# Adding the weighted scan states to y: one unit per GpSimd instruction, or two

## The chip, the cores and the metric

The kernel runs on one core of one Trainium2 chip. The metric is the time of one execution on the device, in microseconds (us). The kernel before took 3660.17 us (median of 3 runs, 3656.47 to 3664.53).

## The reference

One layer on x of shape [8, 512, 512] (batch, sequence L, features D): a feed-forward block, a state-space block (Mamba), and the same feed-forward block again, each added to x, the feed-forward ones by half.

```python
x = x + 0.5 * ffn(layernorm(x))
x = x + mamba(layernorm(x))
x = x + 0.5 * ffn(layernorm(x))
# ffn: h = silu(x @ w_gate) * (x @ w_up); of each 4 neighbours of h the 2 largest by magnitude stay; h @ w_down
# mamba, per batch element, E = 1024 channels, N = 16 states:
h = exp(d_l[..., None] * A) * h + (d_l * u_l)[..., None] * b_l[:, None, :]   # over l = 0..511
y_l = einsum('ben,bn->be', h, c_l)
y = (y + u * W_D) * silu(skip);  out = y @ W_out.T
```

The change touches the two lines of the recurrence: h is scanned over l for each channel and state, and y is the sum over the 16 states of h times C.

## The kernel before

**Tiling.** Features stand on the 128 partitions and the 512 positions along the free axis, so a tile is 128x512 float32. The 1024 channels are 8 tiles e = 0..7, worked in two halves of 4 (HE = 4). A *unit* is one tile e and one state n: one scan over 512 positions. There are 64 units in a half, 128 in a batch element, 1024 in all, numbered u = 0..1023; within a half u runs over e fastest, so 4 units in a row belong to the four tiles of one state.

**A unit passes through four engines.** ScalarE writes exp(delta*A) to a PSUM bank `decay[u % 2]` (L838). GpSimd multiplies du by the row B into `scan_in` (L1322, `scan_input`). VectorE scans (L1201, `scan`), in place in the `decay` bank, and multiplies the states by the row C into `scan_out` (L1211, `times_c`). GpSimd adds that to the tile `y[:, e, :]` (L1333, `sum_states`). `scan_in` and `scan_out` are rings of RING = 4 tiles.

**What orders them.** Semaphores count finished units: `decay_ready`, `input_ready`, `state_ready` (scan done), `weighted_ready` (times C done), `sum_ready` (added to y). `scan_input(u)` waits for the scan of u-4 (its ring tile is free), `times_c(u)` waits for the sum of u-4, ScalarE's exponential of u waits for `times_c(u-2)`. On GpSimd the queue is `scan_input(u)`, `sum_states(u-4)`, `scan_input(u+1)`, `sum_states(u-3)`, and so on; GpSimd does little else between the first unit and the last.

**Beside it** TensorE runs the 512 products of the feed-forward blocks (L621 to L623: three matmuls for high and low parts) with "side jobs" between them: down-projections (L713, L697 to L702), the counting of the 2-of-4 choice (L684), projections of the Mamba block (L728 to L730, L741), means and variances. A plan in Python fixes all orders beforehand in *ticks*; `place_units` spreads the units over the ticks by the other work that VectorE has there. VectorE's own queue in a tick is: up to a quarter of the tick's units, then residual and selection work (L1158, L1168, L1176, L1186), and so on; within a quarter it is scan(u), times_c(u), scan(u+1), with other work between the last scan and its times_c.

**VectorE lines with both inputs in SBUF** also matter: `zlo` (L1134) and `xlo` (L1140), four in a row; the scaling of the normalised input (L1120, L1128); `y` times the gate (L1241, function `gate`, four in a row), which waits until all sums of its half are in; and delta times u (L1248, 2048 columns). The last gate (batch element 7, second half) stands before the last output projection (L741), the last normalisation and the last feed-forward block.

Of the kernel before, what the change touches and what calls it, by code (L numbers as in the profile page):

```python
# [19 lines left out]
B, L, D = 8, 512, 512  # L20
E, N, DT, DC = 1024, 16, 128, 4
I = 2048
P = 128
KD = D // P
KE = E // P
HE = KE // 2
# [4 lines left out]
GROUPS = 2 * N  # L31
HALF = N * HE
UNITS = 2 * HALF
RING = 4
BANKS = 2
EXP_LEAD = 1
MAINS = 2
# [4 lines left out]
ROWS = 3  # L42
# [216 lines left out]
def build(nc, x_in, ffn_w, down_w, mam_w, out_w, wdt_in, wbc_in, wd2_in, small_in, out):  # L259
    f32, r32, bf16 = mybir.dt.float32, mybir.dt.float32r, mybir.dt.bfloat16  # L260
    ALU, ACT = mybir.AluOpType, mybir.ActivationFunctionType
# [4 lines left out]
    with ctx:  # L266
        base_of = {}

        def sb(name, shape, dt=f32):
            base_of[name] = nc.sbuf_base  # L270
            return ctx.enter_context(nc.sbuf_tensor(name, shape, dt))

        def pb(name):
            return ctx.enter_context(nc.psum_tensor(name, [P, L], f32))
# [35 lines left out]
        y = sb("y", [P, KE, L])  # L310
        delta = sb("delta", [P, KE, L])
        du = sb("du", [P, KE, L])
        scan_rows = sb("scan_rows", [P, 2 * ROWS, L])
        rows = [scan_rows[:, 2 * k:2 * k + 2, :] for k in range(ROWS)]
        scan_in = sb("scan_in", [P, RING, L])
        scan_out = sb("scan_out", [P, RING, L])
        db = [scan_in[:, k, :] for k in range(RING)]
        pr = [scan_out[:, k, :] for k in range(RING)]
        cv = [sb(f"cv{k}", [P, L]) for k in range(2)]
        skb = sb("skb", [P, L])  # L320
# [15 lines left out]
        decay = [pb(f"decay{k}") for k in range(BANKS)]  # L336
# [24 lines left out]
        def wait_job(eng, key):  # L361

            eng.wait_ge(sem["side_ready"], index[key] + 1)

        def wait_selected(eng, s, j):

            wait_read(eng, ("win", s, j))
# [10 lines left out]
        def last_down(i):  # L378

            return ("down", EDGE[i], KD - 1)  # L380
# [445 lines left out]
        def _(act):  # L826
# [87 lines left out]
            def member_high(i, j):  # L914

                s = EDGE[i]
                if i:
                    wait_job(act, last_down(i - 1))
                if i == AHEAD_OF_SCANS:
                    act.wait_ge(sem["state_ready"], B * UNITS)  # L920
                    act.wait_ge(sem["sum_ready"], B * UNITS)
                wait_selected(act, s, j)
                nc.scalar.activation(hhi[:, j, :], h[s % 2][:, j, :], ACT.Copy).then_inc(sem["member_high_ready"], 1)  # L923

            def down_high(i, t):

                q = KD * i + t
                act.wait_ge(sem[f"down_loaded_{t}"], 16 * (EDGE[i] + 1))
                if q >= ROWS:
                    wait_job(act, ("down", EDGE[(q - ROWS) // KD], (q - ROWS) % KD))  # L930
                if i == AHEAD_OF_SCANS:
                    act.wait_ge(sem["sum_ready"], B * UNITS)
                nc.scalar.activation(wparts[q % ROWS][:, 0], wdown[t][:], ACT.Copy).then_inc(sem["down_high_ready"], 1)

            def copy_quarters(key):
# [165 lines left out]
        def _(dve):  # L1101
# [96 lines left out]
            def scan(u):  # L1198
                dve.wait_ge(sem["decay_ready"], u + 1)
                dve.wait_ge(sem["input_ready"], u + 1)  # L1200
                nc.vector.tensor_tensor_scan(decay[u % BANKS][:], decay[u % BANKS][:], db[u % RING][:], 0.0, ALU.mult,  # L1201
                                             ALU.add).then_inc(sem["state_ready"], 1)

            def times_c(u):
                m = u // HE
                if u % HE == 0:
                    dve.wait_ge(sem[f"rows_loaded_{m % ROWS}"], 16 * (m // ROWS + 1))
                dve.wait_ge(sem["state_ready"], u + 1)
                if u >= RING:
                    dve.wait_ge(sem["sum_ready"], u - RING + 1)  # L1210
                nc.vector.tensor_tensor(pr[u % RING][:], decay[u % BANKS][:], rows[m % ROWS][:, 1, :], ALU.mult).then_inc(sem["weighted_ready"], 1)  # L1211

            def begin(units):
# [20 lines left out]
                ins.then_inc(read_of(key) if k == DC - 2 else sem["conv_step"], 1)  # L1234

            def gate(b, half):
                dve.wait_ge(sem["sum_ready"], UNITS * b + HALF * (half + 1))
                dve.wait_ge(sem[f"skip_loaded_{half}"], 16 * (b + 1))
                for k in range(HE):
                    e = HE * half + k  # L1240
                    nc.vector.tensor_tensor(y[:, e, :], y[:, e, :], delta[:, gates_in(b, half).start + k, :],  # L1241
                                            ALU.mult).then_inc(sem["gated_ready"], 1)
# [67 lines left out]
        @block.gpsimd  # L1310
        def _(pool):
            def scan_input(u):
                b, v = divmod(u, UNITS)
                half, v = divmod(v, HALF)
                e, m = HE * half + v % HE, u // HE
                if v == 0:
                    pool.wait_ge(sem["du_ready"], 2 * b + half + 1)
                if u % HE == 0:
                    pool.wait_ge(sem[f"rows_loaded_{m % ROWS}"], 16 * (m // ROWS + 1))
                if u >= RING:  # L1320
                    pool.wait_ge(sem["state_ready"], u - RING + 1)
                nc.gpsimd.tensor_tensor(db[u % RING][:], du[:, e, :], rows[m % ROWS][:, 0, :], ALU.mult).then_inc(sem["input_ready"], 1)  # L1322

            def sum_states(u):
                b, v = divmod(u, UNITS)
                half, v = divmod(v, HALF)
                e = HE * half + v % HE
                if v == 0:
                    pool.wait_ge(sem["first_term_ready"], HE * (2 * b + half + 1))
                pool.wait_ge(sem["weighted_ready"], u + 1)  # L1330
                if v >= HE:
                    pool.wait_ge(sem["sum_ready"], u - HE + 1)
                nc.gpsimd.tensor_tensor(y[:, e, :], y[:, e, :], pr[u % RING][:], ALU.add).then_inc(sem["sum_ready"], 1)  # L1333

            def member_low(i, j):

                pool.wait_ge(sem["member_high_ready"], 4 * i + j + 1)
                nc.gpsimd.tensor_tensor(hlo[:, j, :], h[EDGE[i] % 2][:, j, :], hhi[:, j, :], ALU.subtract).then_inc(sem["member_split_ready"], 1)  # L1338

            def down_low(i, t):  # L1340

                w = wparts[(KD * i + t) % ROWS]
                pool.wait_ge(sem["down_high_ready"], KD * i + t + 1)
                nc.gpsimd.tensor_tensor(w[:, 1], wdown[t][:], w[:, 0], ALU.subtract).then_inc(sem["down_split_ready"], 1)

            nc.gpsimd.memset(ones[:], 1.0 / D).then_inc(sem["const_ready"], 1)
            nc.gpsimd.memset(pick[:], 0.0).then_inc(sem["const_ready"], 1)
            pool.wait_ge(sem["const_ready"], 2)
            for k in range(4):
                nc.gpsimd.memset(pick[2 * N * k:2 * N * k + 1, :], 1.0).then_inc(sem["const_ready"], 1)  # L1350
            pool.wait_ge(sem["const_ready"], 6)
            nc.gpsimd.memset(eps[:, 0:1], EPS).then_inc(sem["const_ready"], 1)
            nc.gpsimd.memset(eps[:, 1:2], EPS * EPS).then_inc(sem["const_ready"], 1)
            for k, sign in enumerate((1.0, -1.0)):
                nc.gpsimd.memset(signs[:, k, :], sign).then_inc(sem["const_ready"], 1)
                pool.wait_ge(sem["const_ready"], 2 * k + 9)
                nc.gpsimd.affine_select(signs[:, k, :], signs[:, k, :], pattern=[[-1, P]], compare_op=ALU.is_equal, fill=0.0, base=0,
                                        channel_multiplier=1).then_inc(sem["const_ready"], 1)
            nc.gpsimd.memset(fold[:], 0.0).then_inc(sem["const_ready"], 1)
            for k in range(4):  # L1360
                pool.wait_ge(sem["const_ready"], 13 + k)
                nc.gpsimd.affine_select(fold[:], fold[:], pattern=[[-1, 2 * N]], compare_op=ALU.not_equal, fill=1.0, base=-2 * N * k,
                                        channel_multiplier=1).then_inc(sem["const_ready"], 1)
            for tick in range(plan.ticks):
                if tick == STARTS[0]:
                    wait_job(pool, last_down(AHEAD_OF_SCANS - 1))
                for i, j in edge_members(tick):
                    member_low(i, j)
                for i, t in edge_weights(tick):
                    down_low(i, t)  # L1370
                for u in plan.units_at[tick]:
                    scan_input(u)
                    if u >= RING:
                        sum_states(u - RING)
                if tick == STARTS[B] - 1:
                    for u in range(B * UNITS - RING, B * UNITS):
                        sum_states(u)


def _tiles(v):  # L1380
# [36 lines left out]
```

## Time and profile before

| | before |
|---|---|
| median of 3 runs | 3660.17 us (3656.47 to 3664.53) |
| the profiled execution's own time | 3661.65 us |
| its span, first to last instruction | 3659.9 us |
| mean granted TensorE clock | 0.976 of full |
| TensorE matmul busy | 92% |
| VectorE busy | 83% |
| GpSimd busy | 74% |
| ScalarE busy | 56% |

The profile is one execution; its time is 1.5 us above the median. Scans run from about 300 to 3467 us; outside that GpSimd is nearly idle, so that within it its share is higher than the 74% of the whole. A matmul's recorded end is modelled, so that the share of TensorE is not a share of its peak. An instruction of an engine may be recorded as beginning before the one ahead of it has ended, by some hundredths of a microsecond.

### The profile page before, as it was taken

How to read it: one execution, taken by the hardware profiler on the slowest of the kernel's cores; microseconds unless marked ns; L12 is line 12 of the kernel's file. 1: busy time of each engine (PE TensorE's matmuls, PEld its weight loads, DVE VectorE, ACT ScalarE, POOL GpSimd, SP SyncE). 2: the span in 40 equal slices, each digit the busy share in tenths (PEclk: the TensorE clock that was granted, in tenths of full speed). 3: DMA queues.
4: the chain of work that ended last, by engine and by line, in shares of the span. 5: the costliest groups of instructions: out<-in, count | busy, mean ns of one | idle time of the engine just before them, and what ended most of it. 6: DMA issues, size and time to landing. Idle time of an engine off the chain costs nothing. (4 is left out here: it accounts for less than half of the span.)

```text
span 3659.9 us, 40068 instructions
## 1 busy us (share of the span) xinstructions
PE 3383.1 (92%) x11967; PEld 2131.8 (58%) x12032; DVE 3041.4 (83%) x3572; ACT 2060.4 (56%) x2803; POOL 2694.2 (74%) x2141
## 2 busy tenths in 40 slices
PE   8999999999999999899999999888988999898889
PEld 5775556556655665556555565556545565455466
DVE  5546888788889889898988899998989998989823
ACT  4546556557565664556555675656565665454332
POOL 1316776777888778787787788878988978989813
PEclk9999999999999999999999999999999999999999
DMA  9656556656656666466665575556645566546433
GB/s 350 212 187 191 159 203 210 217 164 216 206 170 216 187 219 216 150 205 206 190 201 178 188 232 185 180 163 214 222 125 207 167 219 202 175 150 187 129 109 104
DMA packets 243477, 696.51 MB, mean 190 GB/s; under 512 B 23536, under 2 KB 23792, under 8 KB 233584
## 3 DMA queue, kind: packets, MB, share of 16 engines
q1 hardware_dynamic: 173632, 559.72, 44.3%
q10 hardware_dynamic: 69632, 134.23, 14.2%
q8 instruction: 99, 1.62, 0.2%
q14 instruction: 114, 0.93, 0.1%
HBM read 619.94 MB, written 76.55 MB: 190 GB/s over the span
## 5 line engine op out<-in xcount | busy, mean ns | idle before, releaser
L1322 POOL TENSOR_TENSOR scan_in<-du,scan_rows 128x512 f32<-128x512 f32 x1024 | 1323.2, 1292 | 544.6 <-DVE decay L1201 456.1
L1333 POOL TENSOR_TENSOR y<-y,scan_out 128x512 f32<-128x512 f32 x1024 | 1351.4, 1320 | 104.7 <-DVE scan_out L1211 103.8
L1201 DVE TENSOR_TENSOR_SCAN decay<-decay,scan_in 128x512 f32<-128x512 f32 x1024 | 1252.2, 1223 | 147.9 <-ACT decay L838 137.0
L838 ACT ACTIVATE decay<-delta,aneg 128x512 f32<-128x512 f32 x1024 | 698.5, 689 | 1016.2 <-DVE scan_out L1211 1012.9
L621 PE MATMUL main<-zhi,wunit 128*128 128x512 f32 x2048 | 913.7, 446 | 129.8 <-ACT h L862 92.5
L623 PE MATMUL main<-zhi,wunit 128*128 128x512 f32 x2048 | 825.4, 403 | 0.0
L622 PE MATMUL main<-zlo,wunit 128*128 128x512 f32 x2048 | 824.5, 403 | 0.0
L713 PE MATMUL side<-h,wdown 128*128 128x512 f32 x1760 | 798.8, 598 | 8.4 <-DVE res_r L1186 3.3
L1211 DVE TENSOR_TENSOR scan_out<-decay,scan_rows 128x512 f32<-128x512 f32 x1024 | 702.7, 686 | 27.9
L621 PEld LDWEIGHTS main<-zhi,wunit 128*128 128x128 f32 x2048 | 394.6, 193 | 325.0 <-ACT h L862 131.0
L713 PEld LDWEIGHTS side<-h,wdown 128*128 128x128 f32 x1760 | 335.1, 192 | 374.6 <-issue 346.9
L622 PEld LDWEIGHTS main<-zlo,wunit 128*128 128x128 f32 x2048 | 396.1, 193 | 121.4 <-issue 37.3
L623 PEld LDWEIGHTS main<-zhi,wunit 128*128 128x128 f32 x2048 | 394.9, 193 | 97.0
L728 PE MATMUL side<-xhi,wmam 128*128 128x512 f32 x512 | 238.7, 466 | 43.7 <-DVE cv L1232 18.5
L1338 POOL TENSOR_TENSOR hlo<-h,hhi 128x512 fp32r<-128x512 f32 x36 | 48.4, 1367 | 282.4 <-ACT hhi L923 282.4
L838 ACT ACT_TABLE_LOAD x193 | 247.6, 1283 | 4.0 <-ACT skb L987 0.5
L741 PE MATMUL side<-y,wmam 128*128 128x512 f32 x512 | 232.2, 597 | 9.8 <-DVE y L1241 4.3
L1168 DVE TENSOR_TENSOR cmp<-ab,mag 128x512 bf16<-128x512 f32 (+2 forms) x192 | 232.5, 1211 | 10.2 <-ACT mag L871 8.9
L1158 DVE TENSOR_TENSOR h<-main,h 128x512 f32<-128x512 f32 x256 | 173.9, 679 | 53.6 <-PE main L623 53.6
L1176 DVE SCALAR_TENSOR_TENSOR h<-side,h 128x512 f32<-128x512 f32 x256 | 165.1, 681 | 60.7 <-PE side L684 60.5
L871 ACT ACTIVATE mag<-h 128x512 f32<-128x512 f32 x192 | 113.2, 589 | 179.7 <-DVE cmp L1168 118.0
L684 PE MATMUL side<-cmp,signs 128*128 128x512 bf16 x703 | 180.4, 391 | 33.0 <-DVE cmp L1168 14.5
(105 smaller groups left out, 3261.9 us busy)
## 6 DMA issues: line engine op xcount, KB each, us to landing
wunit<-hl_dram SPq DMA_DIRECT2D x480, 512.0 KB, 4.1
scan_rows<-bc_dram ACTq DMA_DIRECT2D x256, 512.0 KB, 5.5
wdown<-down_w_dram SPq DMA_DIRECT2D x256, 256.0 KB, 3.0
wmam<-mam_dram SPq DMA_DIRECT2D x128, 512.0 KB, 4.2
hl_dram<-wunit SPq DMA_DIRECT2D x32, 512.0 KB, 3.7
skip_dram<-skb SPq DMA_DIRECT2D x64, 256.0 KB, 4.2
delta<-skip_dram SPq DMA_DIRECT2D x16, 1024.0 KB, 8.1
wmam<-wout_dram SPq DMA_DIRECT2D x32, 512.0 KB, 4.4
```

The costliest lines, as they stand in the source:

```text
L621: nc.tensor.matmul(main[n % MAINS][:], hi[:, k, :], zhi[:, k, :], start=(k == 0), stop=False)
L622: nc.tensor.matmul(main[n % MAINS][:], hi[:, k, :], zlo[:, k, :], start=False, stop=False)
L623: mm = nc.tensor.matmul(main[n % MAINS][:], lo[:, k, :], zhi[:, k, :], start=False, stop=(k == KD - 1))
L713: mm = nc.tensor.matmul(bank[:], wdown[t][:, j, :], h[s % 2][:, j, :], start=(j == 0), stop=(j == 3))
L728: nc.tensor.matmul(bank[:], w[:, k, :], xhi[:, k, :], start=(k == 0), stop=False)
L741: mm = nc.tensor.matmul(bank[:], w[:, odd * KD + t, :].bitcast(f32), y[:, e, :], start=(c + odd == 0), stop=(c + odd == 2))
L838: nc.scalar.activation(decay[u % BANKS][:], delta[:, e, :], ACT.Exp, scale=aneg[:, e, n:n + 1]).then_inc(sem["decay_ready"], 1)
L1168: nc.vector.tensor_tensor(cmp[:, first:first + j, :], ab[:, 0:j, :], mag[:].unsqueeze(1).broadcast_to([P, j, L]), ALU.is_ge).then_inc(sem[ ...
L1201: nc.vector.tensor_tensor_scan(decay[u % BANKS][:], decay[u % BANKS][:], db[u % RING][:], 0.0, ALU.mult, ALU.add).then_inc(sem["state_read ...
L1211: nc.vector.tensor_tensor(pr[u % RING][:], decay[u % BANKS][:], rows[m % ROWS][:, 1, :], ALU.mult).then_inc(sem["weighted_ready"], 1)
L1322: nc.gpsimd.tensor_tensor(db[u % RING][:], du[:, e, :], rows[m % ROWS][:, 0, :], ALU.mult).then_inc(sem["input_ready"], 1)
L1333: nc.gpsimd.tensor_tensor(y[:, e, :], y[:, e, :], pr[u % RING][:], ALU.add).then_inc(sem["sum_ready"], 1)
```

## The change

GpSimd adds the weighted states of two units, which lie in neighbouring tiles of `scan_out`, to two neighbouring tiles of `y` in one instruction of 1024 columns. `sum_ready` now counts pairs, so each wait on it is halved. `scan_input` stays one instruction per unit. The GpSimd queue is now: `scan_input(u)` and `scan_input(u+1)` for an even u, then the sum of units u-4 and u-3.

```diff
-RING = 4
+INPUTS, RING = 4, 4
+
+LAG = 2
...
-        scan_in = sb("scan_in", [P, RING, L])
+        scan_in = sb("scan_in", [P, INPUTS, L])
...
             def times_c(u):
...
                 if u >= RING:
-                    dve.wait_ge(sem["sum_ready"], u - RING + 1)
+                    dve.wait_ge(sem["sum_ready"], (u - RING) // 2 + 1)
...
             def gate(b, half):
-                dve.wait_ge(sem["sum_ready"], UNITS * b + HALF * (half + 1))
+                dve.wait_ge(sem["sum_ready"], (UNITS * b + HALF * (half + 1)) // 2)
...
-            def sum_states(u):
+            def sum_states(p):
+
+                u = 2 * p
                 b, v = divmod(u, UNITS)
                 half, v = divmod(v, HALF)
-                e = HE * half + v % HE
+                e, k = HE * half + v % HE, u % RING
                 if v == 0:
                     pool.wait_ge(sem["first_term_ready"], HE * (2 * b + half + 1))
-                pool.wait_ge(sem["weighted_ready"], u + 1)
+                pool.wait_ge(sem["weighted_ready"], u + 2)
                 if v >= HE:
-                    pool.wait_ge(sem["sum_ready"], u - HE + 1)
-                nc.gpsimd.tensor_tensor(y[:, e, :], y[:, e, :], pr[u % RING][:], ALU.add).then_inc(sem["sum_ready"], 1)
+                    pool.wait_ge(sem["sum_ready"], p - HE // 2 + 1)
+                nc.gpsimd.tensor_tensor(y[:, e:e + 2, :], y[:, e:e + 2, :], scan_out[:, k:k + 2, :], ALU.add).then_inc(sem["sum_ready"], 1)
...
                 for u in plan.units_at[tick]:
                     scan_input(u)
-                    if u >= RING:
-                        sum_states(u - RING)
+                    if u % 2 == 1:
+                        if u // 2 >= LAG:
+                            sum_states(u // 2 - LAG)
                 if tick == STARTS[B] - 1:
-                    for u in range(B * UNITS - RING, B * UNITS):
-                        sum_states(u)
+                    for p in range(B * UNITS // 2 - LAG, B * UNITS // 2):
+                        sum_states(p)
```

## Rows read from the trace of the kernel before

**Rows 1.** The page: busy time by engine; GpSimd's busy tenths in 40 slices.
```profile
PE 3383.1 (92%) x11967; PEld 2131.8 (58%) x12032; DVE 3041.4 (83%) x3572; ACT 2060.4 (56%) x2803; POOL 2694.2 (74%) x2141
...
POOL 1316776777888778787787788878988978989813
```
**Rows 2.** Waits, whole span: who waited for whom, total us, times, longest us.
```profile
ACT decay L838 <- DVE scan_out L1211: 1012.9, 636, 6.7
POOL scan_in L1322 <- DVE decay L1201: 456.1, 216, 12.6
...
POOL y L1333 <- DVE scan_out L1211: 103.8, 101, 4.5
...
DVE decay L1201 <- POOL scan_in L1322: 10.8, 5, 7.9
...
DVE y L1241 <- POOL y L1333: 0.8, 1, 0.8
```
**Rows 3.** Busy us (and count) by engine, 2600 to 2700 us; then clock, DMA.
```profile
2600.00:2700.00 100.00, 85.01 (x262) 46.78 (x262) 92.53 (x105) 56.65 (x79) 98.22 (x80) 0.94 0.54 166
```
**Rows 4.** The page's groups: GpSimd's two lines; busy, mean ns, idle before.
```profile
L1322 POOL TENSOR_TENSOR scan_in<-du,scan_rows 128x512 f32<-128x512 f32 x1024 | 1323.2, 1292 | 544.6 <-DVE decay L1201 456.1
L1333 POOL TENSOR_TENSOR y<-y,scan_out 128x512 f32<-128x512 f32 x1024 | 1351.4, 1320 | 104.7 <-DVE scan_out L1211 103.8
```
**Rows 5.** Timeline of GpSimd near 2674 us: start, duration (us), instruction.
```profile
2673.47 1.33 POOL L1322 TENSOR_TENSOR scan_in<-du,scan_rows 128x512 f32<-128x512 f32 x1
2674.70 1.33 POOL L1333 TENSOR_TENSOR y<-y,scan_out 128x512 f32<-128x512 f32 x1
2675.93 1.34 POOL L1322 TENSOR_TENSOR scan_in<-du,scan_rows 128x512 f32<-128x512 f32 x1
```
**Rows 6.** Groups of GpSimd's instructions: the smallest that write 32 columns.
```profile
L1362 POOL TENSOR_SCALAR_AFFINE_SELECT fold<-fold 128x32 f32<-128x32 f32 x4 | 0.8, 212 | 0.6
...
L1346 POOL MEMSET ones<- 128x32 f32 x1 | 0.1, 124 | 0.3 <-POOLq L1409 0.3
```
**Rows 7.** Timeline of VectorE near 2674 us: units 746 and 747.
```profile
2673.72 0.69 DVE L1211 TENSOR_TENSOR scan_out<-decay,scan_rows 128x512 f32<-128x512 f32 x1
2674.90 1.23 DVE L1201 TENSOR_TENSOR_SCAN decay<-decay,scan_in 128x512 f32<-128x512 f32 x1 [0.50 <-POOL scan_in L1322]
```
**Rows 8.** Timeline near 1878 us: times_c of unit 484, sum of unit 481.
```profile
1878.17 0.69 DVE L1211 TENSOR_TENSOR scan_out<-decay,scan_rows 128x512 f32<-128x512 f32 x1
...
1878.28 1.27 POOL L1333 TENSOR_TENSOR y<-y,scan_out 128x512 f32<-128x512 f32 x1
```
**Rows 9.** Timeline of GpSimd at the end of the scans.
```profile
3465.09 1.26 POOL L1333 TENSOR_TENSOR y<-y,scan_out 128x512 f32<-128x512 f32 x1 [0.94 <-DVE scan_out L1211]
3466.95 1.26 POOL L1333 TENSOR_TENSOR y<-y,scan_out 128x512 f32<-128x512 f32 x1 [0.61 <-DVE scan_out L1211]
```
**Rows 10.** The chain that ended last, from the last sum on: start, us, what.
```profile
3466.95 1.27 POOL y L1333
...
3468.25 0.70 DVE y L1241
...
3469.09 15.67 PE side L741 x32
```
**Rows 11.** VectorE lines with two SBUF inputs: group means (ns), and least durations.
```profile
L1134 DVE TENSOR_TENSOR zlo<-zm,zhi 128x512 fp32r<-128x512 f32 x64 | 56.7, 945 | 0.9 <-ACT zhi L897 0.7
L1241 DVE TENSOR_TENSOR y<-y,delta 128x512 f32<-128x512 f32 x64 | 53.3, 892 | 10.2 <-DMA delta<-skip_dram 9.4 <-POOL y L1333 0.8
...
L1248 DVE TENSOR_TENSOR du<-delta,du 128x2048 f32<-128x2048 f32 x16 | 46.6, 2912 | 10.0 <-ACT y L1022 10.0
...
L1134 DVE TENSOR_TENSOR zlo<-zm,zhi x64: 677/684/3437, 24.5 to 3502.5; 128x512 fp32r<-128x512 f32 x64
...
L1248 DVE TENSOR_TENSOR du<-delta,du x16: 2279/2418/5659, 294.6 to 3211.5; 128x2048 f32<-128x2048 f32 x16
```
**Rows 12.** Timeline, one gate (L1241) from 1392.52 us: GpSimd beside it.
```profile
1392.09 1.29 POOL L1333 TENSOR_TENSOR y<-y,scan_out 128x512 f32<-128x512 f32 x1
...
1393.34 1.72 POOL L1322 TENSOR_TENSOR scan_in<-du,scan_rows 128x512 f32<-128x512 f32 x1
...
1395.02 1.71 POOL L1333 TENSOR_TENSOR y<-y,scan_out 128x512 f32<-128x512 f32 x1
```

More of the change, by code:

```diff
@@ L314, in build @@
         rows = [scan_rows[:, 2 * k:2 * k + 2, :] for k in range(ROWS)]
-        scan_in = sb("scan_in", [P, RING, L])
+        scan_in = sb("scan_in", [P, INPUTS, L])
         scan_out = sb("scan_out", [P, RING, L])
-        db = [scan_in[:, k, :] for k in range(RING)]
+        db = [scan_in[:, k, :] for k in range(INPUTS)]
         pr = [scan_out[:, k, :] for k in range(RING)]
@@ L920, in member_high @@
                     act.wait_ge(sem["state_ready"], B * UNITS)
-                    act.wait_ge(sem["sum_ready"], B * UNITS)
+                    act.wait_ge(sem["sum_ready"], B * UNITS // 2)
                 wait_selected(act, s, j)
@@ L931, in down_high @@
                 if i == AHEAD_OF_SCANS:
-                    act.wait_ge(sem["sum_ready"], B * UNITS)
+                    act.wait_ge(sem["sum_ready"], B * UNITS // 2)
                 nc.scalar.activation(wparts[q % ROWS][:, 0], wdown[t][:], ACT.Copy).then_inc(sem["down_high_ready"], 1)
@@ L1200, in scan @@
                 dve.wait_ge(sem["input_ready"], u + 1)
-                nc.vector.tensor_tensor_scan(decay[u % BANKS][:], decay[u % BANKS][:], db[u % RING][:], 0.0, ALU.mult,
+                nc.vector.tensor_tensor_scan(decay[u % BANKS][:], decay[u % BANKS][:], db[u % INPUTS][:], 0.0, ALU.mult,
                                              ALU.add).then_inc(sem["state_ready"], 1)
@@ L1319, in scan_input @@
                     pool.wait_ge(sem[f"rows_loaded_{m % ROWS}"], 16 * (m // ROWS + 1))
-                if u >= RING:
-                    pool.wait_ge(sem["state_ready"], u - RING + 1)
-                nc.gpsimd.tensor_tensor(db[u % RING][:], du[:, e, :], rows[m % ROWS][:, 0, :], ALU.mult).then_inc(sem["input_ready"], 1)
-            def sum_states(u):
+                if u >= INPUTS:
+                    pool.wait_ge(sem["state_ready"], u - INPUTS + 1)
+                nc.gpsimd.tensor_tensor(db[u % INPUTS][:], du[:, e, :], rows[m % ROWS][:, 0, :], ALU.mult).then_inc(sem["input_ready"], 1)
+            def sum_states(p):
+                u = 2 * p
                 b, v = divmod(u, UNITS)
                 half, v = divmod(v, HALF)
-                e = HE * half + v % HE
+                e, k = HE * half + v % HE, u % RING
                 if v == 0:
                     pool.wait_ge(sem["first_term_ready"], HE * (2 * b + half + 1))
-                pool.wait_ge(sem["weighted_ready"], u + 1)
+                pool.wait_ge(sem["weighted_ready"], u + 2)
                 if v >= HE:
-                    pool.wait_ge(sem["sum_ready"], u - HE + 1)
-                nc.gpsimd.tensor_tensor(y[:, e, :], y[:, e, :], pr[u % RING][:], ALU.add).then_inc(sem["sum_ready"], 1)
+                    pool.wait_ge(sem["sum_ready"], p - HE // 2 + 1)
+                nc.gpsimd.tensor_tensor(y[:, e:e + 2, :], y[:, e:e + 2, :], scan_out[:, k:k + 2, :], ALU.add).then_inc(sem["sum_ready"], 1)
             def member_low(i, j):
@@ L1372, in _ @@
                     scan_input(u)
-                    if u >= RING:
-                        sum_states(u - RING)
+                    if u % 2 == 1:
+                        if u // 2 >= LAG:
+                            sum_states(u // 2 - LAG)
                 if tick == STARTS[B] - 1:
-                    for u in range(B * UNITS - RING, B * UNITS):
-                        sum_states(u)
+                    for p in range(B * UNITS // 2 - LAG, B * UNITS // 2):
+                        sum_states(p)
 def _tiles(v):
```

## The prediction, made before the changed kernel was run

> **What bounds the kernel now.** I read the busy shares first, then the waits, then a stretch where GpSimd has no idle time, then the chain at the end. TensorE is busy 92% of the span and VectorE 83%; GpSimd has 74% of the whole, but eight or nine tenths of many slices while scans run [rows 1]. The question is who waits for GpSimd, for only that can be given back. Nearly nobody: VectorE waited 10.8 us for `scan_input`, 7.9 of it in one piece (the first unit), and 0.8 us at one gate. The other way round GpSimd waited 456.1 us for scans and 103.8 us for weighted states [rows 2]. So GpSimd is a follower with slack, and the kernel goes by TensorE and VectorE, which wait for each other in turns. The exception is a burst like 2600 to 2700 us, where GpSimd is busy 98.22 of 100 us, VectorE 92.53 and TensorE only 85.01 [rows 3]: there GpSimd runs back to back and VectorE begins to wait for it by half a microsecond a unit [rows 7].
>
> **Part 1: one instruction instead of two.** 1024 sums of 1320 ns recorded [rows 4] become 512 pairs. GpSimd's records overlap a little, so I take the spacing of starts: 1.23 us from a product to a sum and again to the next product [rows 5]. Two sums cost 2.46 us. The columns stay, so what a pair saves is at most the fixed part of one instruction. No row shows 1024 columns on GpSimd; I bound the fixed part by the smallest instructions, 124 ns for a memset of 32 columns and 212 ns for a select of 32 [rows 6], and by zero from below. A pair therefore costs 2.25 to 2.46 us. I take 2.34 (0.12 saved), by the memset, since a select does more per column. That is 512 x 0.12 = 61 us less GpSimd time, and by itself it is worth nothing, since its cover is GpSimd's own 560 us of waiting [rows 2]. I see nothing against a small loss either (a two-tile pattern may cost some hundredths more), but more than 2.46 would need a slower column rate, for which there is no sign. The Trainium skill (GPSIMD Engine Reference, section 3.1) gives 4497 ns for a tensor_tensor of 2048 float32 columns; with the 1287 ns that the median record of 512 has, its pair would be 1.07 us longer than a single, a saving of some 0.2 us, and the sums below would fall by about 1 us. No run here shows it.
>
> **Part 2: the queue is coarser.** Before, `times_c(u)` needed `scan_input(u)` and the sum of u-4 ahead of it in GpSimd's queue. Now, for an even u, it needs `scan_input(u+1)` and the whole pair u-4, u-3. For an odd u the same sum as before is needed, and it stands at the same place. For an even u the thing to read is therefore: did `times_c(u)` start before the sum of u-3 had ended? If so, the new wait would bite by the difference, less what was saved since GpSimd last stood idle. Behind the waiting `times_c` on VectorE's queue stand the next scan and the residual work, and behind its `weighted_ready` ScalarE's exponential of u+2, which waits on it already (1012.9 us in all [rows 2]).
> I went through the 510 even units so (the k-th record of L1211 is unit k-1, and likewise on L1333). The median margin is 5.0 us. It is negative for 12 units, in three bursts: units 220 and 222 near 1035 us (0.8 us at most), 482 and 484 near 1876 us, and 738 to 752 near 2670 us. The two larger ones in rows: `times_c(484)` started at 1878.17 while the sum of 481 ended at 1878.28 + 1.27 = 1879.55, so 1.4 us late [rows 8]; `times_c(746)` at 2673.72 [rows 7] while the sum of 743 ended at 2674.70 + 1.33 = 2676.03, so 2.3 us [rows 5]. The lateness of a burst counts once, at its worst unit, not per unit. Against it stands the saving: GpSimd had run without a gap since 1844.9, about 7 pairs before unit 484, 0.8 us saved, 0.6 left; near 2674 it had run since 2594.5, but with the new order it catches up on the way, so I count 9 of 16 pairs, 1.1 us, and add 0.5 for a sum that was pushed behind an earlier pause: 1.7 left. At 1035 us the saving covers all. TensorE has 15 idle us of 100 in the late burst and VectorE 7.5 [rows 3], so it is VectorE that sets the pace and the delay passes on in full; near 1876 perhaps half. **Sum: +2 us**, between 0 (saving 0.21) and about 10 (saving 0, see the rivals).
>
> **Part 3: the end.** The last gate waits for the last sum, and this is on the chain that ends last: sum 3466.95, gate 3468.25, output projection 3469.09 [rows 10]. GpSimd stood idle before the last two sums, waiting for VectorE [rows 9], so the last pair can't start earlier than today's last sum and lasts 2.34 instead of 1.23: **+1.1 us**, with 1.0 to 1.23 as its bounds. Nothing covers it; TensorE has no other work there. The other 15 gates waited for no sum [rows 2].
>
> **Part 4: who holds the read port.** VectorE's lines with both inputs in SBUF are drawn out where GpSimd runs beside them: `zlo` 945 ns in the mean against a least 677, the gate 892 against about 678, delta times u 2912 against 2279 [rows 11]. Over these three: 64 x 0.268 + 64 x 0.214 + 16 x 0.633 = 41 us of VectorE time. The form is alternation: the gate at 1392.52 waits for the sum in progress; the product after it and the next sum are stretched to 1.7 us and each holds up a further step of the gate [rows 12]. With pairs a step that meets a sum may wait 2.3 instead of 1.2 us. But in such a place VectorE has finished unit v and the queue runs dry after the sum of v. If v is even, the sum of v isn't there any more (it waits for v+1) and its collision goes; if v is odd, a pair is there. Of the 28 collisions with a sum in these lines I count 15 with an even number. So one half is doubled and the other removed: **0 us**, bounds -8 (odd ones unchanged, half of some 17 us passed on) and +8 (even ones not removed, half of the doubling passed on).
> The Trainium skill (SBUF — State Buffer, section "SBUF: two separate sides") states the rule behind this: the port pair that VectorE and GpSimd share is an exclusive lock, held for the whole instruction, also against a VectorE instruction with two SBUF inputs. The trace agrees, by the rows just read, and by the rule alone a longer instruction speaks against this change.
>
> **Part 5: nothing.** The halved counts on `sum_ready` in ScalarE's waits (L919, L931) come after the last scan and lie behind the last gate. Odd products come 1.23 us earlier in the queue; their consumers wait only in the late burst.
>
> **Sum.** 2 + 1.1 + 0 = 3.1 us on the profiled execution's 3661.65, 3664.8. That execution stood 1.5 us above the median, so the forecast for a median is 3663.3, 3663 rounded.
>
> **Rivals.**
> *A, the pair saves nothing and the coupling bites.* At 2.46 us a pair the three bursts cost their raw 0.8 + 1.4 + 2.3 = 4.5 us. Moreover each sum of an even unit that fills a pause of VectorE today stands after the pause, 1.23 us of queue more at the start of a burst; about eight further bursts have margins of 0.2 to 0.7 us on even units and would lose about 0.8 each, 6.4. With 1.2 at the end: 12 us, **3672**, slower. It decides from a spacing of about 2.42 us for a pair. For it: VectorE is nearly saturated in late bursts. Against it: an instruction surely has some fixed cost.
> *B, the lock.* Collisions with pairs cost double and the even ones don't go, since bursts are no longer where they were: +6 on the forecast, **3669**, slower. For it: the alternation is plain in the rows. Against it: the parity count.
> *C, less contention.* The odd collisions stay as they are where GpSimd is behind anyway (the total backlog is what VectorE waits for), the even ones go, and the half-microsecond waits of the late burst end because GpSimd is 0.12 us quicker a pair: -8 - 2.9 + 1.1, about -10, **3650**, faster. For it: GpSimd's queue does hold less. Against it: most of VectorE's delay is covered by waits on TensorE.
> *D, the pair isn't one instruction* (two records of 512 columns in a row): then A's time.
>
> **Chances.** Forecast 0.66, A and D 0.13, B 0.11, C 0.10. A measurement of this kernel can tell about 0.2% (7.3 us) from no change: faster is below 3652.8, slower above 3667.5. The forecast's cases lie within, A, D and B above, C below: faster 0.10, same 0.66, slower 0.24. The range is 3654 to 3673: upward it takes in B and A, downward it stops short of C.
>
> **What would show each step.** The pair's record: 1024 columns, x512, spaced 2.34 us to the next product (part 1). A new wait of VectorE's L1211 for GpSimd's L1333, of a few us, near 2674 us (part 2). The last gate starting 2.3 instead of 1.3 us after the last weighted state (part 3). The means of L1134, L1241 and L1248 near those of before, with longer single ones (part 4). GpSimd's wait for scans should shrink or grow by little, its busy time fall by some 60 us. Wrong would make it: a pair of over 2.42 us, or a loss of VectorE time in the bursts after 3300 us, where nothing is idle to take it up.

## The result, and the profile after

The changed kernel took 3676.27 us (median of 5 runs, 3675.73 to 3679.36) against 3661.27 us (median of 5 runs of the kernel before, 3656.47 to 3664.53). The ratio is 1.0045, 95% interval 1.0034 to 1.0055. That is 15.0 us slower in the medians and 16 by the ratio, where 3 us and no measurable change had been forecast, and above the range of 3654 to 3673.

The profiled execution took 3679.36 us, 17.7 more than the one of before. The page's busy line, and its groups for GpSimd (busy us, mean ns of one | idle before it, what ended most of it), answer to [rows 1, 4]:

```profile
PE 3390.1 (92%) x11967; PEld 2137.3 (58%) x12032; DVE 3043.6 (83%) x3572; ACT 2061.4 (56%) x2803; POOL 2605.8 (71%) x1629
...
L1324 POOL TENSOR_TENSOR scan_in<-du,scan_rows 128x512 f32<-128x512 f32 x1024 | 1307.8, 1293 | 669.6 <-DVE decay L1203 583.2
...
L1337 POOL TENSOR_TENSOR y<-y,scan_out 128x1024 f32<-128x1024 f32 x512 | 1239.9, 2422 | 84.8 <-DVE scan_out L1213 84.6
```

GpSimd did its part: 88 us less busy by its records, and it now waits 583.2 us for scans instead of 456.1. VectorE is busy only 2.2 us longer. The loss is on TensorE: 7.0 us more busy, and 10.7 us more idle (span less busy, 276.8 before, 287.5 after). It is busy longer with the same 11967 matmuls because more of them ran at the lower of its two clock levels: the mean granted clock of the two profiled executions is 0.976 and 0.972 of full.

The waits (who for whom, total us, times, longest) answer to [rows 2], and the groups of VectorE's two-input lines to [rows 11]:

```profile
POOL scan_in L1324 <- DVE decay L1203: 583.2, 250, 13.5
...
DVE scan_out L1213 <- POOL y L1337: 5.1, 9, 1.2
...
DVE y L1243 <- POOL y L1337: 1.9, 1, 1.9
```
```profile
L1136 DVE TENSOR_TENSOR zlo<-zm,zhi 128x512 fp32r<-128x512 f32 x64 | 59.5, 990 | 0.9 <-ACT zhi L899 0.7
L1243 DVE TENSOR_TENSOR y<-y,delta 128x512 f32<-128x512 f32 x64 | 57.2, 953 | 9.0 <-DMA delta<-skip_dram 7.2 <-POOL y L1337 1.9
...
L1250 DVE TENSOR_TENSOR du<-delta,du 128x2048 f32<-128x2048 f32 x16 | 41.0, 2562 | 10.1 <-ACT y L1024 10.1
```

The new wait of part 2 is there, 5.1 us in 9 pieces. `zlo` and the gate are drawn out more than before (990 ns against 945, 953 against 892), delta times u less (2562 against 2912). In VectorE time that nearly cancels over these three groups (2.8 + 3.9 - 5.6 us), as part 4 said. Three places show what it does to the other engines. First a gate whose last unit ahead, 771, is odd: VectorE before, then VectorE and GpSimd after (start, duration in us):

```profile
2762.52 2.54 DVE L1241 TENSOR_TENSOR y<-y,delta 128x512 f32<-128x512 f32 x4
```
```profile
2774.82 3.65 DVE L1243 TENSOR_TENSOR y<-y,delta 128x512 f32<-128x512 f32 x4
...
2773.72 2.39 POOL L1337 TENSOR_TENSOR y<-y,scan_out 128x1024 f32<-128x1024 f32 x1
```

Before, the sum ahead ended 0.2 us into the gate and cost it nothing; the pair, begun at 2773.72, ends at 2776.11, 1.3 us into it, and the gate takes 1.1 us longer. The next products of TensorE came 1.1 us later. Second, the four `zlo` after unit 511, also odd: they took 4.35 us before and 5.19 after, and TensorE's wait for them (who for whom, us, times, longest; 1963 to 1977 us before, 1968 to 1982 after) more than doubled:

```profile
PE main L621 <- DVE zlo L1134: 0.7, 1, 0.7
```
```profile
PE main L623 <- DVE zlo L1136: 1.6, 1, 1.6
```

Third, a delta times u whose last unit ahead, 356, is even, before and after:

```profile
1479.26 4.77 DVE L1248 TENSOR_TENSOR du<-delta,du 128x2048 f32<-128x2048 f32 x1 [1.12 <-ACT y L1022]
1483.95 1.22 DVE L1201 TENSOR_TENSOR_SCAN decay<-decay,scan_in 128x512 f32<-128x512 f32 x1
```
```profile
1480.98 3.44 DVE L1250 TENSOR_TENSOR du<-delta,du 128x2048 f32<-128x2048 f32 x1 [1.25 <-ACT y L1024]
1485.38 1.23 DVE L1203 TENSOR_TENSOR_SCAN decay<-decay,scan_in 128x512 f32<-128x512 f32 x1 [0.96 <-ACT decay L840]
```

The sum of the even unit is gone from beside it and it is 1.33 us shorter. The next scan then waits 0.96 us for ScalarE: most of what was gained is idle time. Right behind that VectorE waits 2.72 us for TensorE, whose granted clock in these 15 us was 0.77 (1477 to 1492 us), against 1.00 in the kernel before. That dip doesn't come from the shorter instruction: in e7 below, which has the same pairs and a delta times u of 3.46 us here, the clock of this stretch is 1.00 and the 2.72 us are not there.

Over all 43 places of e4 below, place by place, the time by which VectorE is drawn out (what a place takes above the least, 2.49 us for four instructions in a row and 2.28 us for one of 2048 columns; of the scaling only the latter counts) sums to 21.3 us behind odd units and 23.1 behind even ones in the kernel before, and to 34.5 and 14.3 in the changed kernel. So the odd half grew to 1.6 times its size and the even half lost two fifths: behind an even unit a product can still be met, and where GpSimd is behind, the end of an earlier pair (both at the `zlo` after unit 234).

### The profile page after: what moved, and what is told of

The parts are those of the page before. It is cut to its first block and busy times, and to the rows that moved or that the text cites. A ratio compares the mean times of both kernels' runs of the same rounds, so it can differ in the third digit from the quotient of the medians.

```text
span 3677.6 us, 39076 instructions
## 1 busy us (share of the span) xinstructions
PE 3390.1 (92%) x11967; PEld 2137.3 (58%) x12032; DVE 3043.6 (83%) x3572; ACT 2061.4 (56%) x2803; POOL 2605.8 (71%) x1629
## 5 line engine op out<-in xcount | busy, mean ns | idle before, releaser
L1324 POOL TENSOR_TENSOR scan_in<-du,scan_rows 128x512 f32<-128x512 f32 x1024 | 1307.8, 1293 | 669.6 <-DVE decay L1203 583.2
L1337 POOL TENSOR_TENSOR y<-y,scan_out 128x1024 f32<-128x1024 f32 x512 | 1239.9, 2422 | 84.8 <-DVE scan_out L1213 84.6
```

What stands on the lines that cost most here:

```text
L1324: nc.gpsimd.tensor_tensor(db[u % INPUTS][:], du[:, e, :], rows[m % ROWS][:, 0, :], ALU.mult).then_inc(sem["input_ready"], 1)
L1337: nc.gpsimd.tensor_tensor(y[:, e:e + 2, :], y[:, e:e + 2, :], scan_out[:, k:k + 2, :], ALU.add).then_inc(sem["sum_ready"], 1)
```

## The experiments

All ratios are to the kernel before on the same chip, with 95% intervals. What is compared is mostly a pattern of three things: the order of GpSimd's queue (product, sum, product, sum; or two products, two sums), the instruction (two of 512 columns or one of 1024), and whether GpSimd stands back while VectorE has two-input work.

**e1: the new order with two instructions.**
```diff
-                nc.gpsimd.tensor_tensor(y[:, e:e + 2, :], y[:, e:e + 2, :], scan_out[:, k:k + 2, :], ALU.add).then_inc(sem["sum_ready"], 1)
+                nc.gpsimd.tensor_tensor(y[:, e, :], y[:, e, :], pr[k][:], ALU.add)
+                nc.gpsimd.tensor_tensor(y[:, e + 1, :], y[:, e + 1, :], pr[k + 1][:], ALU.add).then_inc(sem["sum_ready"], 1)
```


> The changed kernel with each pair's sum issued as two instructions of 512 columns behind each other; the order of GpSimd's queue (two products, then two sums) and the counting of sum_ready in pairs stay. It undoes only the length of the instruction. Theory L (length: a GpSimd instruction of 2.33 us beside VectorE lines with two SBUF inputs makes each such meeting cost 1.1 us more, and the added idle time of TensorE is followed by more time at the lower clock): near the kernel before, 3658 to 3665 us, means of L1136 (zlo) and L1243 (gate) back to about 945 and 892 ns. Theory Q (the coarser queue: times_c of an even unit waits for two products and two sums): stays at 3673 to 3680 us, or is longer, since GpSimd also loses the 0.13 us a pair that it had saved.

Measured: 3685.38 us, ratio 1.0070 (1.0058 to 1.0083). Theory L falls: with the short instruction the kernel is slower still, as theory Q had allowed. The groups of its two-input lines, and its new wait:

```profile
L1136 DVE TENSOR_TENSOR zlo<-zm,zhi 128x512 fp32r<-128x512 f32 x64 | 60.6, 1006 | 0.9 <-ACT zhi L899 0.7
L1243 DVE TENSOR_TENSOR y<-y,delta 128x512 f32<-128x512 f32 x64 | 58.2, 968 | 9.4 <-DMA delta<-skip_dram 7.4 <-POOL y L1338 2.0
```
```profile
DVE scan_out L1213 <- POOL y L1338: 15.0, 27, 1.3
```

`zlo` and the gate are drawn out as much as with pairs, so it isn't the length of the instruction. In the new order the sum of v-1 waits until the weighted state of v is there too (both kernels wait for `weighted_ready` of u + 2 first), and after an odd v two sums are pending, in one piece or in two. At the `zlo` after unit 161 that costs the same: one instruction of 2.86 us in the changed kernel, two of 1.77 and 1.76 in e1, against a single 1.77 in the kernel before (before, changed, e1):

```profile
863.73 1.77 DVE L1134 TENSOR_TENSOR zlo<-zm,zhi 128x512 fp32r<-128x512 f32 x1
```
```profile
862.44 2.86 DVE L1136 TENSOR_TENSOR zlo<-zm,zhi 128x512 fp32r<-128x512 f32 x1
```
```profile
864.11 1.77 DVE L1136 TENSOR_TENSOR zlo<-zm,zhi 128x512 fp32r<-128x512 f32 x1
...
865.80 1.76 DVE L1136 TENSOR_TENSOR zlo<-zm,zhi 128x512 fp32r<-128x512 f32 x1
```

Merging the two sums into one instruction is in itself a gain here (1.0070 to 1.0045, 9 us), some of it in the waits of `times_c` just shown.

**e3: two instructions only where VectorE has two-input work next** (two pairs ahead of each such place, with the two lines of e1; all other sums are pairs).

> The changed kernel with pairs everywhere except at the two pairs ahead of each place where VectorE has a line with two SBUF inputs (zlo, xlo, scaling, gate, delta times u): there the sum is two instructions of 512 columns. Theory L: most of the loss goes, 3659 to 3667 us, though most pairs stay pairs. Theory Q: as the changed kernel, 3673 to 3680 us.

Measured: 3672.52 us, ratio 1.0035 (1.0023 to 1.0048), hardly apart from the changed kernel and just under what theory Q gave. `zlo` stayed at 1001 ns and the gate at 957, for the reason just given. In its profiled execution the mean granted clock was 0.976 and TensorE's busy time 3382.3 us, as before the change: its loss is idle time of TensorE alone.

**e4: the kernel before, GpSimd stands back.** I call it a *meeting* when a GpSimd instruction runs beside a VectorE line with two SBUF inputs. For each place with such lines, `passed` holds under the number of the last unit ahead of it the semaphore and count that say it is over:
```diff
+            if tick in plan.ffn_start:
+                passed.setdefault(early, []).append(("normed_ready", KD * (plan.ffn_start[tick] + 1)))
...
                 for u in plan.units_at[tick]:
+                    for name, count in passed.get(u - 4, []):
+                        pool.wait_ge(sem[name], count)
                     scan_input(u)
```
(There are 43 such places; those in ticks without units are left out. It is the same for xlo, the scaling lines, the gate and delta times u; `early` and `late` are the last units of the tick's first and second quarter. The wait holds back the product, and behind it in the queue the sum.)

> The kernel before (single sums) with one wait more in GpSimd's queue at each of those places: GpSimd starts the product after the last unit ahead of the place only when VectorE's two-input lines there are done, so that they do not meet. Theory L: the 41 us that zlo, gate and delta times u are drawn out shrink to under 15 us, and since a part of them is on the path of TensorE the time falls by 5 to 25 us, to 3635 to 3655 us, with less time at the lower clock. Theory Q says nothing of it; if meetings are hidden anyway, the time stays within 3654 to 3668 us or rises because GpSimd falls behind.

**e5: the changed kernel with the same waits.**

> The changed kernel (pairs) with the same added waits in GpSimd's queue. Theory L: with the meetings gone the length of the sum matters no more, so it comes within about 4 us of the kernel before with these waits, 1.1 us of it at the last gate. Theory Q: it stays 12 to 18 us slower than the kernel before with these waits.

Measured: e4 3644.29 us, ratio 0.9960 (0.9948 to 0.9973), 14 us faster than before. e5 3648.31 us, 0.9966 (0.9954 to 0.9978): 4 us above e4 in the medians, 28 us faster than the changed kernel. So the waits are worth twice as much in the changed kernel, and with them the change costs next to nothing. In e4 the 41 us of `zlo`, gate and delta times u fell to 11, as expected; the granted clock of its profiled execution did not rise with it (0.976, as before). In e5:

```profile
L1262 DVE TENSOR_TENSOR y<-y,delta 128x512 f32<-128x512 f32 x64 | 45.3, 767 | 8.6 <-DMA delta<-skip_dram 6.7 <-POOL y L1356 1.9
L1155 DVE TENSOR_TENSOR zlo<-zm,zhi 128x512 fp32r<-128x512 f32 x64 | 42.1, 718 | 0.9 <-ACT zhi L918 0.7
```

**e6: e1 with the waits** closes the table: new order, short instructions, no meetings.

> e1 (order of the changed kernel, each pair as two instructions of 512 columns) with the added waits of e4. Theory M (meetings: the new order leaves two sums, not one, behind the last unit ahead of a two-input line of VectorE): most of the 27 us of e1 go, to 3648 to 3656 us, 4 to 12 above e4. Theory Q (the coarser queue: times_c of an even unit waits for two products and two sums): e1's loss stays beside e4, 3665 to 3672 us.

Measured: 3659.78 us, ratio 0.9999 (0.9990 to 1.0008), between the two expectations. The waits win 0.7% back, but beside e4 0.4% (14 us) is left. I read most of it as the coarser queue, since `times_c` now waits for sums, which in e4 it never does:

```profile
DVE scan_out L1232 <- POOL y L1357: 17.2, 31, 1.3
```

With pairs the same wait is 5.3 us in 10 pieces (e5). A small part may be two-input lines still drawn out (13 us over all places in e6, 10 in e4). So with two sums of 2.46 us the new order costs 14 us beside e4, and with a pair of 2.32 us next to nothing. Together:

| ratio to before | without waits | GpSimd stands back |
|---|---|---|
| product, sum, product, sum | 1 | 0.9960 (e4) |
| two products, two short sums | 1.0070 (e1) | 0.9999 (e6) |
| two products, a pair (the change) | 1.0045 | 0.9966 (e5) |

**e7 and e8: the changed kernel, waits only after odd or only after even units** (`if u % 2 == 1`, or 0, on the added wait).

> The changed kernel with the added waits only at the places whose last unit ahead has an odd number (20 of 43), where a whole pair is pending. Theory M with the parity of the prediction: nearly all of the gain of e5 is here, 3648 to 3658 us. If the meetings that count are spread over both parities, 3655 to 3668 us.

> The changed kernel with the added waits only at the places whose last unit ahead has an even number (23 of 43), where no pair is pending and at most a product is met. Theory M with parity: little gain, 3670 to 3678 us. If both parities count, 3660 to 3670 us.

Measured: e7 3647.37 us, ratio 0.9969 (0.9958 to 0.9979), the whole gain of e5; e8 3673.17 us, 1.0037 (1.0025 to 1.0050), nearly none of it. What the waits win back in the changed kernel lies at the places after an odd unit. The gate after unit 771 isn't one of them: it stands in a tick without units and still takes 3.6 us in e5 and e7, against 2.54 before the change, so that its 1.1 us are likely a part of the 4 us by which e5 stays above e4.

**e11 and e12: the same two halves on the kernel before.** They ask what each half was worth there.

> The kernel before (single sums) with the added waits only at the 23 places of even number, the meetings that the changed kernel loses by itself. The prediction booked their loss as a gain of about 8 us that makes up for the odd ones. Were that right, this kernel is 6 to 10 us faster than before, 3650 to 3654 us. If they are hidden, it is within 3 us of before, 3656 to 3662 us.

> The kernel before with the added waits only at the 20 places of odd number. If the even meetings are hidden, all of e4's gain of 14 us is here, 3643 to 3650 us; if both parities count alike, half of it, 3650 to 3655 us.

Measured: e11 3662.13 us, ratio 1.0003 (0.9994 to 1.0012); e12 3647.59 us, 0.9968 (0.9955 to 0.9980). The even meetings, of which the change removes two fifths, were worth nothing that can be measured in the kernel before (the interval leaves room for 2 us of gain); the odd ones, which it makes 1.6 times as heavy, were worth 12 us of e4's 14. The traces show that the waits did their work in both: the time drawn out at the even places fell from 23.1 to 1.9 us in e11, that at the odd ones from 21.3 to 2.2 in e12. In e11 the odd places rose from 21.3 to 24.9 us, so a little of its gain may have gone there. At the delta times u of unit 356, e11 shows the gain turning into idle time:

```profile
1474.73 2.34 DVE L1267 TENSOR_TENSOR du<-delta,du 128x2048 f32<-128x2048 f32 x1 [1.12 <-ACT y L1041]
1479.13 1.23 DVE L1220 TENSOR_TENSOR_SCAN decay<-decay,scan_in 128x512 f32<-128x512 f32 x1 [2.07 <-ACT decay L857]
```

**e10: e7 with the waits at zlo, xlo and the gate only** (12 places instead of 20).

> e7 with its waits only at zlo, xlo and the gate (12 places of odd number), not at the scaling lines and delta times u (8). Theory P (the meetings that count are those on TensorE's way: its products wait for zlo, its projections for xlo and the gate): nearly all of e7's gain, 3646 to 3656 us. If the place of a meeting does not matter, about half of it, 3658 to 3666 us.

Measured: 3648.07 us, ratio 0.9969 (0.9957 to 0.9980), as e7. The waits at the scaling lines and delta times u add nothing; twelve places are enough. That doesn't prove that the place is what counts: of the 34.5 us drawn out at the 20 odd places, these twelve hold 30.2 and the other eight only 4.3.

**e9: e4 with the waits also at places in ticks without units.**

> e4 (single sums, added waits) with the waits also at the places in ticks that hold no unit of their own, which e4 leaves out. Theory M: a little faster than e4, 3636 to 3644 us, with the mean of the gate near its least of 678 ns. If what is left is hidden, within 2 us of e4; if GpSimd falls behind by the waits, slower than e4.

Measured: 3641.68 us, ratio 0.9958 (0.9945 to 0.9972), not to be told from e4; the gate's mean came to 727 ns, not to its least. The best of the versions run are these two, single sums with the waits; both beat the kernel before and the changed one.

## Why the prediction was wrong

**What bounds the kernel:** right. GpSimd's 88 us gave nothing back; they appear as wait (583.2 us for scans). One sign was wrong: this wait was to shrink or grow by little, and it grew by 127 us.

**Part 1, the pair's price: right.** Forecast 2.34 us and 0.12 saved. After the change, GpSimd in a stretch without gaps (start, duration in us; "x2" is two products in a row):

```profile
3442.09 2.52 POOL L1324 TENSOR_TENSOR scan_in<-du,scan_rows 128x512 f32<-128x512 f32 x2
3444.59 2.35 POOL L1337 TENSOR_TENSOR y<-y,scan_out 128x1024 f32<-128x1024 f32 x1
3446.91 2.53 POOL L1324 TENSOR_TENSOR scan_in<-du,scan_rows 128x512 f32<-128x512 f32 x2
```

From the pair's start to the next, 2.32 us, 0.14 less than two singles at 1.23. The other estimate there, some 0.2 us saved, is a little too high. Rival D is out: the page has 512 records of 1024 columns.

**Part 2, the coarser queue, +2 us: right in size.** e5 stands 4 us above e4 in the medians (0.06% by the ratios, less than their intervals), 1.1 of it at the last gate and, likely, as much at the gate after unit 771. The new waits of `times_c` for sums stand where the prediction put them: of the nine, one is near 1035 us, two near 1880, five between 2668 and 2693, and only one elsewhere. Rival A's time for a pair that saves nothing, 12 us, is what e6 shows beside e4 (14 us). By e6 this rival would have come true without the 0.14 us a pair, so the forecast of part 2 hung on a number that the prediction could only bound by 0 and 0.21.

**Part 3, the last gate, +1.1 us: right.** In the chain that ended last the pair now stands with 2.35 us where [rows 10] has 1.27:

```profile
3483.49 2.35 POOL y L1337
3485.86 0.70 DVE y L1243
```

**Part 4, the port, 0 us: this is the step that failed.** The direction was right for both halves: after an odd unit more is met, after an even one less. The share of even collisions (15 of 28) comes out alike in a recount: 35 sums run beside zlo, the gate or delta times u for any time at all, 18 of them even. The sizes were rougher than "doubled" and "removed": 21.3 to 34.5 us, and 23.1 to 14.3. Even so VectorE is busy only 2.2 us longer. What was wrong is to net the two halves and to pass on "half" of each. The even half was worth 0 (e11) and the odd half 12 us (e12), so nothing stood against the growth of the odd one: the odd meetings cost the changed kernel 28 us, all that the waits win there (e7, e5), against 12 of the 14 in the kernel before (e12, e4). The difference, 14 to 16 us, is the loss. Where part 4 has 0, the runs show about +14. My bound of +8 came from the same halving.

Could I have seen it? The trace tells for each place whether TensorE or the next VectorE line waits behind it, and I took the parity from it but not that. But the line alone would not have settled it: in the kernel before, the 11 even places at zlo, xlo and the gate hold 16.2 us drawn out and the 12 odd ones 16.8, and they are worth nothing and some 12 us.

I also gave a wrong reason inside this step. I named the length of the instruction ("a step that meets a sum may wait 2.3 instead of 1.2 us"), and the sentence on the exclusive lock drew the same from it. e1 shows that two short sums in a row cost as much: what counts is how much GpSimd work is released at once by the last `times_c` ahead of the place.

**Rivals.** B (the lock, 3669) had the right sign and place and was too small. Its reason, that the even meetings would not go, is true in part (14.3 of 23.1 us stayed), but they are not what costs: e8, which takes most of them away, wins 3 us by the ratios, less than their intervals. A and C did not come true; C's gain of even meetings is the one that e11 shows to be nothing.

**What stays open.** About 7 us of the profiled difference is matmul time at the lower clock level. Whether it belongs to the change is not shown. e3 has the same granted clock as the kernel before and a ratio of 1.0035; its five runs lie between 3670.8 and 3673.3 us at 0.972 to 0.976; and 17 runs of the kernel before, on one chip, span 0.973 to 0.978. Nor do the runs say why the even meetings are hidden and the odd ones are not; it may be no more than where this plan happens to put 43 places.

## What to carry to other kernels

Grouping two steps of a helper engine into one saves an instruction's fixed part, but it also defers the first step until the second can run, so that more work is released at once. Look at what the neighbour engine does just then: if the two hold each other up, as VectorE's two-input lines and GpSimd did here, the burst lands on it. And don't net gains and losses of an engine's time over the whole kernel: of two halves of 21 and 23 us, one was worth 12 us and the other nothing, and only runs that took away one half at a time told them apart. Making the helper stand back was worth 0.3% in the kernel before at 20 places and 0.4% at all 43; in the changed kernel twelve places gave 0.8%.

## What the runs showed of the hardware

A VectorE instruction with two SBUF inputs and a GpSimd instruction that reads SBUF take turns, whole instruction by whole instruction. The Trainium skill (SBUF — State Buffer, section "SBUF: two separate sides") says so, and these runs agree: beside the pair of 2.74 us after unit 161 one `zlo` takes 2.86 us instead of 0.68, and with the waits of e5 the mean of `zlo` fell from 990 to 718 ns, near its least of 677. What I hadn't expected is that cutting the GpSimd work in two does not help the other side: between four VectorE instructions in a row the pending GpSimd instructions are let in one after another, so that two short sums hold up two of the four. They cost 1006 ns in the mean (e1) where one long one costs 990.
